# Splitting the output product of a fused state-space and expert kernel into three single-pass products

## The reference

```python
h = jnp.concatenate([tok(x), txt(x_txt)], axis=1)          # (32, 68, 256)
xn = layernorm(h)
u = xn @ W_x.T + b_x;  g = sigmoid(xn @ W_g.T + b_g)        # hidden width 512
u = u * g + depthwise_conv3(u) * (1 - g)
dt = clip(mean(softplus(xn @ W_dt.T + b_dt)), 0.001, 2.0)
y = scan over the 68 tokens of a diagonal system with 16 states, driven by u
out = jnp.einsum('blh,dh->bld', y, W_out) + b_out           # contraction over 512
h = h + (layernorm(xn + out) * ln_g + ln_b)
... # then h = h + ffn(layernorm(h)): router, top 2 of 4 experts, w1 (256 x 512), layernorm, relu, w2 (512 x 256)
```

## Time and profile before

| | us |
|---|---|
| median of 3 runs | 524.66 |
| lowest and highest of them | 521.92, 527.88 |
| the profiled execution, its own time | 522.35 |
| its span in the trace | 520.6 |
| lying around the span | 1.75 |

### The profile page before, as it was taken

The page is one execution under the profiler, slowest core; times in us unless marked ns, Lnnn a source line. Parts: engine busy times, 40 slices in busy tenths (PEclk is TensorE's granted clock), DMA queues, the critical chain, the costliest instruction groups (busy, mean ns, idle before and its releaser), DMA issues.

```text
span 520.6 us, 10312 instructions
## 1 busy us (share of the span) xinstructions
PE 448.0 (86%) x3168; PEld 366.3 (70%) x3168; DVE 342.0 (66%) x1063; ACT 299.9 (58%) x669; POOL 172.0 (33%) x373
## 2 busy tenths in 40 slices
PE   8989996895999999987989799999987999999500
PEld 5779865673788878875767587877766888878400
DVE  6875569789895324427777857875584466767275
ACT  3854376579765464246434426767575777878341
POOL 2000000000000000002366667577777755656322
PEclk9999999799799999999989899999998999999955
DMA  8980110000087536935132232213223243333262
GB/s 180 173 232 31 52 30 1 0 2 1 0 213 186 141 88 159 277 92 172 37 97 71 76 88 73 72 54 101 82 85 99 72 124 112 107 90 102 69 202 71
DMA packets 51617, 50.98 MB, mean 98 GB/s; under 512 B 25672, under 2 KB 46188, under 8 KB 50156
## 3 DMA queue, kind: packets, MB, share of 16 engines
q1 hardware_dynamic: 47116, 39.70, 30.0%
q0 software_dynamic: 3552, 9.74, 5.2%
q10 hardware_dynamic: 896, 0.89, 0.6%
HBM read 35.56 MB, written 15.81 MB: 99 GB/s over the span
## 4 chain that ended last, share of the span: by engine, by line
PE 53%; DVE 15%; issue 9%; POOL 8%; ACT 7%; DMA 4%; SPq 2%; POOLq 0%; DVEq 0%; ACTq 0%
PE bank L849 9%; PE bank L1002 7%; PE bank L417 6%; PE bank L419 5%; PE bank L418 5%; PE bank L915 4%; PE bank L869 3%; POOL expert_y L703 2%; POOL sorted_x L652 2%; PE bank L909 2%; PE bank L897 2%; DMA got_b<-expert_y 1%; PE bank L992 1%; DVE spj L1366 1%; DMA expert_y<-ysb,toid 1%
## 5 line engine op out<-in xcount | busy, mean ns | idle before, releaser
L1002 PE MATMUL bank<-w,hr 128*128 x320 | 78.1, 388 | 5.8 <-DVE ysb L1627 3.9
L628 POOL MEMSET ones<- 2x128 f32 x1 | 0.2, 199 | 213.8 <-PE bank L884 213.8
L1002 PEld LDWEIGHTS bank<-w,hr 128*128 128x128 f32 x320 | 58.5, 193 | 14.7 <-issue 8.1
L1200 ACT ACTIVATE hr<-bank,gsel 128x128 f32<-128x128 f32 x160 | 60.1, 458 | 11.8 <-PE bank L992 11.2
L703 POOL DMA_INDIRECT expert_y<-ysb,toid x40 | 43.8, 1095 | 37.1 <-DVE ysb L1627 25.1
L849 PE MATMUL bank<-Tb,U 68*32 68x68 f32 x1024 | 45.9, 359 | 0.0
L652 POOL DMA_INDIRECT sorted_x<-x2s,slot x34 | 33.8, 995 | 30.2 <-DVE slot L1551 21.7
L849 PEld LDWEIGHTS bank<-Tb,U 68*32 68x32 f32 x1024 | 40.6, 139 | 3.3 <-issue 2.5
L1192 ACT ACTIVATE hn<-bank,nmrh,rsh 128x512 f32<-128x512 f32 x40 | 31.1, 777 | 15.2 <-DVE nmrh L1621 13.4
L915 PE MATMUL bank<-Wo,yT 128*128 128x256 f32 x136 | 35.9, 410 | 2.3 <-ACT yT L1015 2.3
L417 PE MATMUL bank<-w_hi,bT_hi 128*128 x80 | 35.1, 438 | 2.1 <-issue 1.0
(11 more groups left out here) (299 smaller groups left out, 1199.5 us busy)
## 6 DMA issues: line engine op xcount, KB each, us to landing
Tb<-ssm_kernels SPq DMA_DIRECT2D x16, 680.0 KB, 7.2
xg<-sorted_x SPq DMA_DIRECT2D x40, 129.0 KB, 2.1
...
```

What stands on the lines that cost most here:

```text
L1002: mm = pe.matmul(bank[6][:, 0:D], hr[:, i % 3, c, :], w2[:, bass.ds(expert[i], 1), c, :].rearrange("p o n -> p (o n)"), start=(c == 0), st ...
L1200: last = act.activation(hr[:, i % 3, c, :], bank[3 + i % 2][:, c * P:(c + 1) * P], ACT.Relu, scale=gsel[:, i, 0, c:c + 1], bias=gsel[:, i, ...
```

## The change

`W_out` and the turned rows are each split into a part rounded to the single-pass type (`float32r`) and the remainder. Each of the four products of a tile becomes three single-pass products by `split3`: high rows with high weights, high rows with low weights, low rows with high weights. The product low with low is left out.

For the weights, a new step `wos` rounds all 1024 elements per partition on ACT (`Wo_hi`) after the last scan product, and DVE subtracts (`Wo_lo`), once. For the rows, ACT's copy now writes the rounded type, and a new step `yT` on DVE subtracts the rounded copy from the bank (`yT_lo`, 512 elements per partition), once per tile. The product waits for `yT_lo` in place of `yT`. To have semaphores left, `ident` and `block_consts` are folded into `consts` and `sort_consts` with higher counts, and `rsh` into DVE's own chain; the instructions there are the same.

```diff
@@ placement of tiles
+("Wo_lo", [P, HC, D], F32R)   behind padr
-yT [P, 2, HC, P]
+yT [P, 2, HC, P] F32R, yT_lo [P, 2, HC, P] F32R
-(hr,) = place(R5, R6, ("hr", [P, 3, HC, P]))
+hr, Wo_hi = place(R5, R6, ("hr", [P, 3, HC, P]), ("Wo_hi", [P, HC, D], F32R))
...
@@ the table of the order
             "act": dict(xb=-58.7, yT=-74.4, ...
-                rs=14.6, b3=27.1, c1w=-31.4, c1s=26.7, c2=40.0, w1s=-176.0),
+                rs=14.6, b3=27.1, c1w=-31.4, c1s=26.7, c2=40.0, w1s=-176.0, wos=-250.0),
-            "dve": dict(out=-68.3, ln1a=-47.5, ...
+            "dve": dict(out=-68.3, yT=-78.0, ln1a=-47.5, ... wos=-250.0),
...
-            if kind == "yT" and 0 < i <= PARTS[1].start:
+            if kind == "yT" and who != "dve" and 0 < i <= PARTS[1].start:
                 late -= 15
...
@@ PE
                 elif kind == "out":
                     ps = bank[out_bank(i)][:, 0:D]
-                    pe.wait_ge(sem("yT"), i + 1)
+                    pe.wait_ge(sem("yT_lo"), i + 1)
+                    pe.wait_ge(sem("Wo_split"), 1)
                     for j in range(HC):
-                        pe.matmul(ps, yT[:, i % 2, j, :], Wo[:, j, :], start=(j == 0), stop=False)
+                        split3(pe, ps, yT[:, i % 2, j, :], yT_lo[:, i % 2, j, :], Wo_hi[:, j, :], Wo_lo[:, j, :], j == 0, False)
...
@@ ACT
+                elif kind == "wos":
+                    act.wait_ge(sem("ssm_mm"), 2 * QN)
+                    copy(Wo_hi[:], Wo[:]).then_inc(sem("Wo_hi"), 1)
...
@@ DVE
             for kind, i in order("dve"):
-                if kind == "out":
+                if kind == "wos":
+                    dve.wait_ge(sem("Wo_hi"), 1)
+                    dve.tensor_tensor(Wo_lo[:], Wo[:], Wo_hi[:].bitcast(F32), ALU.subtract).then_inc(sem("Wo_split"), 1)
+                elif kind == "yT":
+                    dve.wait_ge(sem("yT"), i + 1)
+                    if i >= 2:
+                        dve.wait_ge(sem("out_mm"), i - 1)
+                    dve.tensor_tensor(yT_lo[:, i % 2].rearrange("p j (t b) -> p j t b", b=B),
+                                      bank[out_bank(i)][:].rearrange("p (t j b) -> p j t b", j=HC, b=B),
+                                      yT[:, i % 2].bitcast(F32).rearrange("p j (t b) -> p j t b", b=B),
+                                      ALU.subtract).then_inc(sem("yT_lo"), 1)
+                elif kind == "out":
```

More of the change, by code:

```diff
@@ L184, in build_kernel @@
         assert AUX >= R2
-        Wo, zjunk, rwt, w1_lo, w1_hi, w2, ong_b, onb_b, ysb, before, beats, ties, ranks, lastk, etab, rowr, toid, padr = place(
+        Wo, zjunk, rwt, w1_lo, w1_hi, w2, ong_b, onb_b, ysb, before, beats, ties, ranks, lastk, etab, rowr, toid, padr, Wo_lo = place(
             AUX, R4, ("Wo", [P, HC, D]), ("zjunk", [P, 2, D]), ("rwt", [E, D]), ("w1_lo", [P, E, DC, HF], F32R),
@@ L188, in build_kernel @@
             ("ties", [P, 2, E, E]), ("ranks", [P, 2, E]), ("lastk", [P, 4, E]), ("etab", [1, 48], I32),
-            ("rowr", [1, 48], I32), ("toid", [P, 8], U32), ("padr", [1, 2, E], I32))
+            ("rowr", [1, 48], I32), ("toid", [P, 8], U32), ("padr", [1, 2, E], I32), ("Wo_lo", [P, HC, D], F32R))
         RAW = AUX + size(HC, D) + size(2, D) + size(D)
@@ L204, in build_kernel @@
         spt, spj = place(R4, R5, ("spt", [P, 4, 512]), ("spj", [P, 2, 512]))
-        yT, r1, h0r, xb, xg, bT_hi, bT_lo, hn = place(
-            R4 + size(P, L), R5, ("yT", [P, 2, HC, P]),
+        yT, r1, h0r, xb, xg, bT_hi, bT_lo, hn, yT_lo = place(
+            R4 + size(P, L), R5, ("yT", [P, 2, HC, P], F32R),
             ("r1", [P, 4, D]), ("h0r", [P, 4, D]), ("xb", [P, 3, D]), ("xg", [P, 4, DX]), ("bT_hi", [P, 2, DC, P], F32R),
-            ("bT_lo", [P, 2, DC, P], F32R), ("hn", [P, 2, HF]))
+            ("bT_lo", [P, 2, DC, P], F32R), ("hn", [P, 2, HF]), ("yT_lo", [P, 2, HC, P], F32R))
         got_a, got_b, acc = place(R4, R4 + size(P, L), ("got_a", [P, DEEP, D]), ("got_b", [P, DEEP, D]), ("acc", [P, DEEP, D]))
@@ L324, in build_kernel @@
             "act": dict(xb=-58.7, yT=-74.4, ln1a=-30.1, h1a=11.8, x2=16.3, x2T=24.4, wts=57.3, b1=-7.7, b2=11.6,
-                rs=14.6, b3=27.1, c1w=-31.4, c1s=26.7, c2=40.0, w1s=-176.0),
+                rs=14.6, b3=27.1, c1w=-31.4, c1s=26.7, c2=40.0, w1s=-176.0, wos=-250.0),
             "pool": dict(h0b=-79.2, h1b=8.2, scat=21.1, table=45.4, b1=-34.7, b4=4.4, c2=60.0),
             "sp": dict(h0in=58.9, load=96.4, gat=73.1, fin=266.4),
-            "dve": dict(out=-68.3, ln1a=-47.5, ln1b=-21.4, h1a=-14.2, x2=2.7, lg=33.6, sel=34.0, rank=44.0,
-                table=50.0, rel=47.7, wts=134.7, b1=-14.6, b2=-3.4, rs=4.5, b4=32.1, c1=-1.9, c2=22.3, w1s=-178.0),
+            "dve": dict(out=-68.3, yT=-78.0, ln1a=-47.5, ln1b=-21.4, h1a=-14.2, x2=2.7, lg=33.6, sel=34.0, rank=44.0,
+                table=50.0, rel=47.7, wts=134.7, b1=-14.6, b2=-3.4, rs=4.5, b4=32.1, c1=-1.9, c2=22.3, w1s=-178.0, wos=-250.0),
             "odd": dict(yT=21.1, xb=8.8, out=17.5, h0in=6.5, x2T=4.3, lgm=8.1, scat=-0.8, gat=18.4, fin=0.3)}
@@ L335, in place_of @@
                 return place_of("sp", "fin", i - i % 2 - 2 * (i // 2 - HEAD) - 1) + i / NT
+            if kind == "wos":
+                return AT[who][kind]
             if kind == "w1s":
@@ L353, in order @@
             for kind in AT[who]:
-                count = NK if kind in BLOCKWISE else NT if kind in BY_TILE else E if kind == "w1s" else 2 if kind in BY_PART else len(FB)
+                count = NK if kind in BLOCKWISE else NT if kind in BY_TILE else E if kind == "w1s" else 1 if kind == "wos" else 2 if kind in BY_PART else len(FB)
                 steps += [(kind, i) for i in range(count) if kind != "regs" or (i - FIRST[block_part(i)]) % 8 == 0]
@@ L627, in _ @@
             pool.wait_ge(sem("c_ps"), len(C_RING))
-            pool.memset(ones2[:].bitcast(F32), 1.0).then_inc(sem("block_consts"), 1)
+            pool.memset(ones2[:].bitcast(F32), 1.0).then_inc(sem("sort_consts"), 1)
             pool.iota(kth[:], pattern=[[1, TAB]], base=0, channel_multiplier=0,
-                      allow_small_or_imprecise_dtypes=True).then_inc(sem("block_consts"), 1)
-            pool.memset(before[:], 1.0).then_inc(sem("block_consts"), 1)
-            pool.wait_ge(sem("block_consts"), 3)
+                      allow_small_or_imprecise_dtypes=True).then_inc(sem("sort_consts"), 1)
+            pool.memset(before[:], 1.0).then_inc(sem("sort_consts"), 1)
+            pool.wait_ge(sem("sort_consts"), 15)
             pool.affine_select(out=before[:], in_=before[:], compare_op=ALU.is_gt, fill=0.0, base=0,
-                                    pattern=[[1, E], [-1, E]], channel_multiplier=0).then_inc(sem("block_consts"), 1)
+                                    pattern=[[1, E], [-1, E]], channel_multiplier=0).then_inc(sem("sort_consts"), 1)
             pool.iota(spare[:], pattern=[[P, NK]], base=2 * N, channel_multiplier=1,
-                      allow_small_or_imprecise_dtypes=True).then_inc(sem("block_consts"), 1)
+                      allow_small_or_imprecise_dtypes=True).then_inc(sem("sort_consts"), 1)
             pool.wait_ge(sem("ssm_mm"), 2 * QN)
             pool.iota(x2s[:, :, D], pattern=[[P, NT]], base=N, channel_multiplier=1,
-                      allow_small_or_imprecise_dtypes=True).then_inc(sem("block_consts"), 1)
-            pool.wait_ge(sem("block_consts"), 6)
+                      allow_small_or_imprecise_dtypes=True).then_inc(sem("sort_consts"), 1)
+            pool.wait_ge(sem("sort_consts"), 18)
             for kind, i in order("pool"):
@@ L731, in _ @@
             warm(bank[0], 16)
-            pe.wait_ge(sem("ident"), 2)
+            pe.wait_ge(sem("consts"), 2)
             for step in A_STEPS:
@@ L1401, in _ @@
             dve.wait_ge(sem("adt"), 1)
-            dve.wait_ge(sem("consts"), 6)
+            dve.wait_ge(sem("consts"), 8)
             for j in range(HC):
```

27 lines of the change are left out of this document (14 added, 13 removed).

## The result

The changed kernel takes 557.75 us (median of 4 runs, 551.24 to 560.25); the kernel before took 523.61 in the same series. The ratio is 1.061, interval 1.056 to 1.066. I had predicted 542 and at most 551: the sign is right and the size is not. Each experiment was measured in a series with the kernel before. The profiled executions of experiments 4 and 8 were disturbed ones, and I take no stage times from them (the expectations of experiments 7 and 10 quote some from experiment 4, which are to be read with that in mind).

A forecast was written before the change was run, and what follows sets the result against it. PE held 53% of the last chain, DVE 15%; products would wait on DVE's nearly full queue. Terms 6.3 + 4.8 + 2.8 + 1.0 + 3.9 - 0.3 = 18.5 us gave 540.9 or 543.2; forecast 542, range 531 to 551.

The forecast's parts named there:

- The bound and the mechanism of the waits: Tile stage: each product waits for a DVE subtraction queued behind other steps; one subtraction in seven hides behind PE.
- product 0: First tile's product: the weights' split and the subtraction let it start at 230.8 in place of 229.80 us.
- the first two rows of the table: First turning to rank 0, forecast +6.3 us; rank 0 to rank 3, forecast +4.8 us.
- Nearly full: DVE in the tile stage: its queue was called nearly full, while the product's operand came from ACT, with room.
- the clock set apart as a rival: Tile stage: half clock adds 1.2 us a product, for half of 14 products 8 us, 549 to 551; chance 0.16.
- Steps 0 to 1 and on: Tiles 0 to 5: time from one product's start to the next, such as 5.46 and 3.99 us.
- Tiles 13 to 16: Around the expert stage's start: tile 13 +2.8, tile 14 +1.0, tile 15 +3.9, tile 16 -0.3 us.
- The product's gain: All 17 tiles: twelve single-pass products take 1.6 against 1.92 us, saving 0.3 us a tile, 5 us at most.
- Faster: Rival: the subtraction is ready when PE gets there, only PE's saving counts, 519 to 521 us; chance 0.06.
- no change: Rival: waits at the start are made up in the expert stage, no change to tell; chance 0.05.
- Slower, but by less: Rival: expert stage absorbs waits of tiles 14 and 15, 534.7 to 537, or waits overlap, down to +6; chance 0.18.

The follow-up runs named there:

- experiment 4: Changed kernel with DVE's row subtraction moved forward in DVE's order for 14 of 17 tiles: 531.93 us, ratio 1.011 to the kernel before.
- experiment 8: Changed kernel with only the subtractions of tiles 13 and 15 moved forward on DVE: 546.41 us, ratio 1.038 to the kernel before.
- experiment 7: experiment 4 with unread PE products (fills) ahead of rank groups 1 to 3 and products 8 to 13 and 15: 525.59 us, ratio 1.002.
- experiment 10: Changed kernel with only the subtractions of tiles 1 to 8 moved forward on DVE: 542.00 us, ratio 1.035 to the kernel before.
- experiment 1: Changed kernel without DVE's row subtraction and PE's wait for it; third pass reuses the high rows: 526.87 us, ratio 1.002.
- experiment 9: experiment 1 plus an equally large DVE subtraction of two halves of Wo, which nobody waits for: 530.07 us, ratio 1.008.
- experiment 5: experiment 1 with unread PE products (fills) ahead of rank groups 1 to 3 and products 9 to 13 and 15: 524.36 us, ratio 0.998.
- experiment 3: Changed kernel with 0 to 24 unread 512-column PE products (fills) ahead of each tile's product: 546.13 us, ratio 1.039.
- experiment 2: Changed kernel with the product unsplit as before, while DVE still subtracts and PE still waits for it: 567.57 us, ratio 1.081.

## Why the prediction was right or wrong

**What was right.** The bound and the mechanism of the waits: the operand of each product now comes from behind other steps in DVE's queue, and PE waits for it 14 times (28.4 us), longest at tiles 13 and 15. Experiments 1, 4 and 9 show it by three ways: without step and wait nothing is lost, with the step elsewhere +5.6, with the step and no wait +4.3. The durations hold: subtraction 0.68 (I had 0.69), twelve passes 1.61 at full clock (I had 1.6), product 0 2.44 us behind the first turning (I had 230.8 - 228.34 = 2.46). And with the clock held up by fills, the first two rows of the table come to +10.6, where my sum had +11.1. "Nearly full" was too strong a word for DVE's queue: DVE was busy 22.2 of 32 us in 228 to 260 us before the change, and 15.9 after it. The late place did the harm, not a lack of room.

**What was wrong: the clock.** The step that failed is the sum's assumption that PE runs the tile stage at full clock, with the clock set apart as a rival, chance 0.16, priced at +8 "for half of the 14 before the expert stage". Steps 0 to 1 and on, which I had at 5.46, 3.99, 5.1, 4.0 and 4.9 us, measured 6.82, 5.42, 6.34, 5.42 and 6.08: my waits, and 1.2 to 1.4 more in each for a product at the lower level. The 1.2 us a product were right. The count was not: products 0 to 5, 8 and 11 ran wholly at the lower level (0.58 us for the first pass, 2.86 to the bias) and product 7 mostly, 8 x 1.25 + 0.9 = 10.9 us before rank group 3. That is most of the 12.1 by which the first two rows of the table exceed mine (23.2 - 11.1), and of the 12.6 by which they exceed those with fills (23.2 - 10.6); in the fills' 6.9 for the first row some 1.0 is their own delay of product 0. I had the earlier trace rows in hand, a stretch at half clock behind a wait of 1.14 us, and a change that put waits like it ahead of nearly every product. That asked for a larger chance than 0.16, and for a price over nearly all of the products. It did not make the case certain: the kernel before also waited 1.27 us ahead of the turning at 239.98 and read 1.00 all through 228 to 260 us, and experiments 1 and 5 show both outcomes behind the same wait. One such wait may leave the clock whole; a row of them did not. How much of the lower level a run gets differs too: of the changed kernel's own runs, one with a mean granted clock of 0.923 had a span of 549.5 us, and those with 0.902 and 0.908 had 556.4 and 555.6.

**Tiles 13 to 16.** I had +7.4 and measured +10.6; experiment 8 prices tiles 13 and 15 at 11.8 together, against my 6.7. The fills of experiment 3 did not change it (+10.9), because they did not bring the clock back here: product 13 still waited 2.85 us, and 15 had none ahead of it. From the end of `h1` to the first block the timeline of the changed kernel shows:

```profile
327.28 0.55 PE L922 MATMUL bank<-bo_hl,ones 2*128 2x256 f32 x1
327.77 0.44 PE L930 MATMUL bank<-ident,x2s 128*128 128x128 f32 x2
...
329.38 0.70 PE L911 MATMUL bank<-ident,y 128*128 128x128 f32 x4
329.85 3.90 PE L899 MATMUL bank<-w_hi 128*128 128x512 f32 x16
```

and that of the kernel before, where the turning and about half of the 16 idle products ran at the lower clock (0.53 to 0.62 in 298 to 302 us):

```profile
299.01 1.13 PE L909 MATMUL bank<-ident,y 128*128 128x128 f32 x4 [1.71 <-DVE r L1471]
299.79 4.92 PE L897 MATMUL bank<-w_hi 128*128 128x512 f32 x16
```

From product 13 to the turning of tile 14 it is 4.95 us (324.43 to 329.38); I had 1.6 + 0.42 + 0.47 = 2.49. Of the 2.46 more, 1.25 are the product at half clock and 1.2 are PE's turning of `x2s` and its router products, which stand between the two in the queue and which I left out, since before the change they ran while PE waited for `r1`. The turning and the fills then took 4.2 us against 5.5 (333.59 - 329.38, 304.54 - 299.01), which gave 1.3 back. 2.8 + 2.5 - 1.3 makes 4.0, and 3.9 was measured. Tile 14 came out at +1.3 (I had +1.0), the start of product 15 at +3.9 behind 14 as I had. From 15 to 16 it is 9.67 us against 8.11, where I had -0.3: product 15 took 2.86 us to its bias instead of 1.92, and the steps behind it (350.10 to 356.91) 6.8 instead of 6.2, the clock being 0.54 in 346 to 352 us. Summed up over the table's rows (33.8 us): my terms stand for 18.5 of them, the router's work that I left out for 1.2, and the lower clock for nearly all of the other 14. Of these 14 the 12.1 of the first two rows are backed by the fills; the rest I only read off the timeline.

**The product's gain.** I took 0.3 us a tile, 5 us in all, from the pace of the earlier trace rows. On PE the twelve passes save that; on the path it came to 2.7 us at equal fills, and to nothing without them (ratio 1.002), and the trace of experiment 1 has the 12 us at half clock in its place. Why the clock fell there is not shown; that a shorter product leaves PE idle sooner is only an argument. The four passes of the Trainium skill (FP8 and Floating Point Precision, TensorE Precision Notes) gave an estimate of 1.44 us for three of them; the trace has 1.61 at full clock, nearer to the row than to the page. At the lower clock the ratio is nearer to that rule: 2.86 to the 3.7 of experiment 2 is 0.77, where it is 1.61 to 1.92, 0.84, at full clock.

**The rivals.** "Faster" and "no change" are ruled out by the ratio of 1.061; DVE did not run ahead of PE, as PE's 14 waits for it show. "Slower, but by less" needed the expert stage to absorb the waits of tiles 14 and 15; from product 16 to the end it is 199.5 us both times, so nothing was given back later. "Slower by more, through the clock" is what happened, at nearly twice its price.
